# Local attention in a two-layer kernel on one core: one probabilities-times-V step per pair of heads, transposed probabilities kept in place of the probabilities, new issue orders

## The reference

```python
x = L0_attn_x
xn = _layernorm(x)
s = _L0_attn_ref(xn, ...)            # four quaternion/spectral sublayers, each with an MLP
g = _silu(_L0_ffn_ref(xn, ...))      # 8 experts, top 2
x = x + s * g
xn = _layernorm(x)
s = _L1_attn_ref(xn, W_qkv, W_out)   # the change is in here
g = _silu(_L1_ffn_ref(xn, ...))      # 32 experts, top 4 in 2 of 4 groups, and a shared one
x = x + s * g
```

```python
sim = jnp.einsum('bhwid,bhwjd->bhwij', bq, bk)      # 128 queries x 256 keys per window
sim = jnp.where(mask, mask_value, sim)
attn = jax.nn.softmax(sim, axis=-1)
out = jnp.einsum('bhwij,bhwjd->bhwid', attn, bv)
```

## Time and profile before

| | value |
|---|---|
| median of 3 runs | 4467.36 us (4463.34 to 4469.44) |
| the profiled execution | 4463.56 us |
| its span (first to last instruction) | 4461.7 us |
| mean granted TensorE clock | 0.967 of full |
| PE busy | 3924.9 us (88%), 18416 instructions |
| DVE busy | 3710.1 us (83%), 10482 |
| ACT busy | 3203.3 us (72%), 7121 |
| POOL busy | 1291.5 us (29%), 1520 |
| DMA, mean over the span | 33 GB/s |

### The profile page before, as it was taken

One profiled execution on the slowest core, in us unless ns is written; L12 is line 12 of the kernel. 1 busy time (PEld: TensorE's weight loads), 2 busy tenths in 40 slices (PEclk: granted clock), 3 DMA queues, 4 the chain that ended last, 5 costly groups with the idle time before them and its releaser, 6 DMA issues. The chain is left out here.

```text
span 4461.7 us, 62568 instructions
## 1 busy us (share of the span) xinstructions
PE 3924.9 (88%) x18416; PEld 2244.7 (50%) x18416; DVE 3710.1 (83%) x10482; ACT 3203.3 (72%) x7121; POOL 1291.5 (29%) x1520
## 2 busy tenths in 40 slices
PE   5668998999989999998999899999998998999978
PEld 3335555555555545555554555545555554554544
DVE  4769898898988889798888988889798888979854
ACT  2447778677776867777777776867777787777756
POOL 0123233222332322233232323322233332223321
PEclk8779999999999999999999999999999999999989
DMA  4011111011111111111111111101111111111100
GB/s 135 15 29 27 27 38 37 25 31 36 30 28 33 33 31 31 29 34 35 30 30 36 26 28 36 39 22 34 33 32 30 32 33 33 31 29 33 36 22 22
DMA packets 144425, 148.05 MB, mean 33 GB/s; under 512 B 27749, under 2 KB 107933, under 8 KB 143961
## 3 DMA queue, kind: packets, MB, share of 16 engines
q1 hardware_dynamic: 144088, 144.06, 12.4%
HBM read 22.32 MB, written 4.19 MB: 6 GB/s over the span
## 5 line engine op out<-in xcount | busy, mean ns | idle before, releaser
L633 POOL TENSOR_TENSOR rot<-rot,sinT 128x512 f32<-128x512 f32 x256 | 336.8, 1316 | 814.7 <-DMA rot<-raw 814.7
L955 DVE TENSOR_TENSOR acc<-acc,tmp 128x512 f32<-128x512 f32 x768 | 559.4, 732 | 8.1
L1387 PE MATMUL bC<-hu,w_d 128*128 128x512 f32 x1056 | 562.8, 615 | 2.8 <-DVE hu L1151 2.6
L605 POOL TENSOR_TENSOR veA<-mvA,epsT 128x2 f32<-128x2 f32 x290 | 83.5, 288 | 1631.7 <-DVE mvA L807 1629.1
L955 DVE TENSOR_TENSOR tmp<-comps 128x512 f32<-128x512 f32 x768 | 539.7, 708 | 7.4
L751 ACT ACTIVATE probs<-probs,nmax 128x256 f32<-128x256 f32 (+1 forms) x1024 | 480.5, 470 | 75.3 <-DVE nmax L1106 72.4
L779 ACT ACTIVATE s_h<-bG 128x512 f32<-128x512 f32 x528 | 314.8, 596 | 193.5 <-PE bG L1370 170.1
L1151 DVE TENSOR_TENSOR hu<-bU,s_h 128x512 f32<-128x512 f32 x528 | 359.7, 681 | 78.5 <-PE bU L1380 67.4
L624 POOL TENSOR_TENSOR comps<-comps 128x255 f32<-128x255 f32 (+1 forms) x384 | 268.7, 703 | 470.6 <-ACT comps L697 470.0
L1106 DVE CUSTOM_DVE_ANT_0 probs<-bT,maskb 128x256 f32<-128x256 f32 (+1 forms) x1024 | 344.9, 383 | 68.3 <-PE bT L1296 67.5
L1277 PE MATMUL bA<-acc,w_fc 128*128 128x256 f32 x1024 | 333.4, 416 | 42.0 <-ACT acc L715 32.5
(11 more groups left out here) (202 smaller groups left out, 8838.5 us busy)
## 6 DMA issues: line engine op xcount, KB each, us to landing
rot<-raw SPq DMA_DIRECT2D x1024, 64.0 KB, 2.0
comps<-comps SPq DMA_DIRECT2D x384, 120.0 KB
x_ld<-in_L_attn_x SPq DMA_DIRECT2D x66, 128.0 KB, 2.2
comps<-comps SPq DMA_DIRECT2D x384, 8.0 KB
out<-sums SPq DMA_DIRECT2D x16, 256.0 KB, 2.2
w_a<-in_L_attn_W_qkv SPq DMA_DIRECT2D x1, 1536.0 KB, 14.4
w_fc<-in_L_attn_fc_w SPq DMA_DIRECT2D x1, 1024.0 KB, 9.5
w_g<-in_L_ffn_w_gate SPq DMA_DIRECT2D x1, 1024.0 KB, 5.6
```

The source lines that it names most:

```text
L633: nc.gpsimd.tensor_tensor(rot[:, i, :], rot[:, i, :], sinT[:, :], ALU.mult).then_inc(sin_part, 1)
L955: V_.tensor_tensor(dst, i0, i1, op).then_inc(ham[h], 1)
L1387: ins = mm(bC[:, :], down, hu[:, :], start=u in (0, UNITS0), stop=u in (UNITS0 - 1, UNITS - 1))
```

## The change

`O` becomes one step per pair over all 512 columns, and the transposes of the reciprocals become a step `RT` of their own with its own bank. There are again 13 bank fillings per pair. `rinv` is one step (128x8 reciprocal, 128x512 spread), ACT's copy of the transposed reciprocals is one 128x512 copy, DVE's product one 128x512 multiplication. The tile `probsT` is gone: ACT writes the transposed probabilities over the probabilities themselves (`in_set`), in the two windows and the head that PE has just transposed. The semaphore `scaled` is gone: DVE waits for `O` on PE and for `RT` on ACT. The matmuls and transposes are the same in number and shape. The strings of all five engines are new.

```diff
-        out += [("rinv", p, 0), ("PT", p, 0), ("PT", p, 1), ("rinv", p, 1), ("O", p, 0), ("PT", p, 2), ("PT", p, 3), ("O", p, 1)]
+        out += [("PT", p, 0), ("PT", p, 1), ("rinv", p), ("PT", p, 2), ("PT", p, 3), ("RT", p), ("O", p)]
...
 ORDER = {
-    "pe": "uuuauabaubautbuuubuttutuuuuuutuuuututttuuuttuuuttaautuatauauuuatuababtuttauauauabubututbtububbut"
+    "pe": "uuuauababuauubtubututuututuuuutuuuuuutuuttutututaatuuuaauuttuuaauababutttauauauauubtbttububbttub"
...
-        probsT = sb("probsT", [P, 2, 4 * WIN])
...
+        def in_set(h, n):
+
+            return probs[:, h, 2 * n:2 * n + 2, :].rearrange("p w n -> p (w n)")
...
                     if t[0] == "PT":
                         t_ready(act, r, t)
                         at = P if t[2] < 2 else 0
-                        copy(probsT[:, t[2] % 2, at:], b[:, at:]).then_inc(t_sem(t), 1)
+                        copy(in_set(t[2] % 2, t[2] // 2)[:, at:], b[:, at:]).then_inc(t_sem(t), 1)
                     if t[0] == "rinv":
-                        w = slice(2 * t[2], 2 * t[2] + 2)
-                        act.wait_ge(rinved, r.b * (2 * HP) + (2 * t[1] + t[2] + 1))
-                        copy(sums[:, w, :].rearrange("p w (h d) -> p w h d", h=2),
-                             rinv[:, w, :].unsqueeze(3).to_broadcast([P, 2, 2, DH])).then_inc(spread, 1)
-                    if t[0] == "O":
+                        act.wait_ge(rinved, r.b * HP + (t[1] + 1))
+                        copy(sums[:, :, :].rearrange("p w (h d) -> p w h d", h=2),
+                             rinv[:, :, :].unsqueeze(3).to_broadcast([P, NW, 2, DH])).then_inc(spread, 1)
+                    if t[0] == "RT":
                         t_ready(act, r, t)
-                        copy(sums[:, 2 * t[2]:2 * t[2] + 2, :].rearrange("p w d -> p (w d)"), b[:, HT:S]).then_inc(scaled, 1)
+                        copy(sums[:, :, :].rearrange("p w d -> p (w d)"), b[:, :]).then_inc(t_sem(t), 1)
...
                     if t[0] == "rinv":
-                        w = slice(2 * t[2], 2 * t[2] + 2)
-                        if t[1:] == (0, 0):
+                        if t[1] == 0:
                             dve.wait_ge(stored, r.b * 16 + 16)
-                        dve.wait_ge(exped, r.b * (NW * HP) + (NW * t[1] + 2 * t[2] + 2))
-                        V_.reciprocal(rinv[:, w, :], rsum[:, w, :]).then_inc(rinved, 1)
+                        dve.wait_ge(exped, r.b * (NW * HP) + (NW * t[1] + NW))
+                        V_.reciprocal(rinv[:, :, :], rsum[:, :, :]).then_inc(rinved, 1)
                     if t[0] == "O":
-                        dve.wait_ge(scaled, r.b * (2 * HP) + (2 * t[1] + t[2] + 1))
-                        V_.tensor_tensor(OT[:, t[1] % 2, t[2] * HT:(t[2] + 1) * HT], b[:, 0:HT],
-                                         sums[:, 2 * t[2]:2 * t[2] + 2, :].rearrange("p w d -> p (w d)"),
+                        t_ready(dve, r, t)
+                        t_ended(dve, r, ("RT", t[1]))
+                        V_.tensor_tensor(OT[:, t[1] % 2, :], b[:, :], sums[:, :, :].rearrange("p w d -> p (w d)"),
                                          ALU.mult).then_inc(t_sem(t), 1)
...
+                    if t[0] == "RT":
+                        pe.wait_ge(spread, r.b * HP + (t[1] + 1))
+                        ins = transposes(b, [sums[:, w, :] for w in range(NW)])
                     if t[0] == "O":
 
-                        tiles = ((2, 1, 0, 2), (1, 0, 0, 1), (3, 3, 1, 1)) if t[2] else ((0, 1, 0, 2), (1, 3, 1, 1))
-                        for n, (key, at, to, wide) in enumerate(tiles):
-                            for h in range(2):
-                                mm(b[h * DH:(h + 1) * DH, to * WIN:(to + wide) * WIN], V[:, key, h, :],
-                                   probsT[:, h, at * WIN:(at + wide) * WIN], start=n == 0, stop=n == len(tiles) - 1)
-                        pe.wait_ge(spread, r.b * (2 * HP) + (2 * t[1] + t[2] + 1))
-                        ins = transposes(b[:, HT:S], [sums[:, 2 * t[2] + w, :] for w in range(2)])
+                        for half, tiles in enumerate((((0, 1, 0, 2), (1, 3, 1, 1)), ((2, 1, 0, 2), (1, 0, 0, 1), (3, 3, 1, 1)))):
+                            for n, (key, at, to, wide) in enumerate(tiles):
+                                for h in range(2):
+                                    ins = mm(b[h * DH:(h + 1) * DH, half * HT + to * WIN:half * HT + (to + wide) * WIN],
+                                             V[:, key, h, :], in_set(h, half)[:, at * WIN:(at + wide) * WIN],
+                                             start=n == 0, stop=n == len(tiles) - 1)
```

More of the change, by code:

```diff
@@ L96 @@
                  "fc0", "fc1", "fc2", "fc3", "mproj"},
-           "t": {"xn1_T", "route1", "q", "k", "V", "S", "PT", "O", "gates1_T", "out", "final_T"},
+           "t": {"xn1_T", "route1", "q", "k", "V", "S", "PT", "RT", "O", "gates1_T", "out", "final_T"},
            "u": {"gate", "weight", "down", "up"}, "r": set()},
@@ L100 @@
                   "prep_T", "gate_T", "gates0_T", "ln2_T", "fc0", "fc1", "fc2", "fc3"},
-            "t": {"xn1_T", "route1", "q", "k", "V", "S", "rinv", "PT", "O", "gates1_T"},
+            "t": {"xn1_T", "route1", "q", "k", "V", "S", "rinv", "PT", "RT", "gates1_T"},
             "u": {"gate", "down"}, "r": {"r0"}},
@@ L141 @@
-    "sp": "aabbabttttaatatbbbttaatatbbbttttaababbtbatt",
+    "pe": "uuuauababuauubtubututuututuuuutuuuuuuutttuttututaatuuuaauuttuuaauababutttauauauauubtbttububbttub"
+          "tuuububtutuutbtabuauttauattattattauttatttuuuuttautatbuabuuattubttbuububbubttuutuutubttubbuabtaut"
+          "auuutatattuatuuatuattuatuttbubtbuataubttbtbtabttbbtatuutttutbuutbubttubttutaatbtttuuutttbuuuuttu"
+          "uuutuuuutttuuuuuttuaubtautbtuttbaubatbaubabaubtabta",
+    "act": "uaabauabaaaabaabtbabbubbbtbtutabubtuttuauttttutattuatattaautaaaaaaataaabaubatbbbuttttuabtbbtutbt"
+           "bbbtubtbbbaatbtattaattttuttttuatbataauaataaaatbaubbtbbuttttatabutbbbtbbttbbbbtubbbataatuataatttt"
+           "tutttatbabatubttbtbaabattaatttaattbattbtbbbubbbbabtabtabbtubtttttutttttuuturttuttttttttabubababa"
+           "babua",
@@ new lines @@
+    "dve": "aubatbutaaubabauaaubabbabauauaubatuauaabatutattatauaabtbaburubbbbbbbrbuaabbaburtauarauaatturaata"
+           "aabbatubatataauaaauabuaabratbbbbbbtbbbbtutttbabattuaubbbbbabtbuaubaaaatatuuaaaaabbtatuutabaaaatb"
+           "uabuaabtbbbabububbbtbbbtbtbubttubaatbatbbuubtatatbbttbtuutaaaaabtabauuatbbbbbaabttbabatttuburrbt"
+           "bauauababauutbabubuttaubbutbatrabaubtbrubautttbtbaa",
+    "pool": "abtaabbbtatttttaabaatabtbbtbatatatabtbtabtbbaabattttatabtabbbbtttab",
+    "sp": "aabbttabttaattabbttbaattabbbttattababatbtbt",
@@ L348, in program @@
         exped = sem("exped")
-        rinved, spread, scaled = sem("rinved"), sem("spread"), sem("scaled")
+        rinved, spread = sem("rinved"), sem("spread")
         y_gated = sem("y_gated")
@@ L1307, in t_part @@
                     builds_on = {"route1": [("xn1_T",)],
-                                 "O": [("V",) + t[1:2]] + [("PT", t[1], 2 * t[-1] + k) for k in range(2)] if t[0] == "O" else [],
-                                 "out": [("O", 2 * t[-1] + k, n) for k in range(2) for n in range(2)] if t[0] == "out" else []}
+                                 "O": [("V",) + t[1:2]] + [("PT", t[1], k) for k in range(4)] if t[0] == "O" else [],
+                                 "out": [("O", 2 * t[-1] + k) for k in range(2)] if t[0] == "out" else []}
                     if t == ("q", 0):
```

## The result

| | before | after |
|---|---|---|
| median, range of four runs | 4468.4 us (4463.3 to 4471.0) | 4432.2 us (4430.1 to 4439.6) |
| ratio of the times, 95% interval | | 0.9923 (0.9906 to 0.9941) |
| span of the profiled execution | 4461.7 us | 4428.7 us |
| granted clock, mean | 0.967 | 0.970 |

The account below looks back on a forecast made before the run. PE was taken as the nearest bound, with DVE's lateness making most of its gaps. PE's 37 us and DVE's 22 us, half let through as 30 us, took 4463.6 to 4434 us; range 4395 to 4487.

Parts of the forecast that it names:

- PE's wait at the product: PE waiting for ACT's copies before the product with V: 56.1 us before, forecast to fall under 20.
- PE gives back 37 us: Two thirds of PE's 56.1 us wait before the product with V, taken as removed PE idle time.
- nothing to see: Rival, chance 0.14: PE's work sets the end and gaps return before other steps; 4463 us, within 9 us.
- PE's work: Matmuls and transposes on PE stay the same, so nothing was taken off PE's work.
- forecast 39.9: Upper-end fall of DVE's busy time from merged reciprocals and products: 148.9 removed less 109.0 added.
- counted 22: DVE's gain in capacity from merged reciprocals and products, 21.8 us by distances between instruction starts, taken as 22.
- ACT at nothing: ACT's merged copies (50.6 us less busy) and saved table loads (23.1 us) costed at nothing, covered by ACT's idle time.
- 18 table loads: Table loads on ACT that the new order saves, at 1.283 us each, 23.1 us.
- The round: A full round taken as 259.9 us from DVE's last steps, 15 to 16 times; about 258 us expected after.
- The slower rival: Chance 0.22: PE waits at RT for ACT's spread, 0.85 us in each of 128 steps, 109 us; 4489 us, or 4507.
- Half of 59 let through: PE's 37 and DVE's 22 us, halved to 30 us because an engine standing less arrives earlier at its next wait.
- A third of 96 us lost: Larger-gain rival, chance 0.18: PE's 56.1 and DVE's 39.9 us count fully, 4368 us, or 4395 with a third lost.

Follow-up runs that it names:

- the second profile: The changed kernel, unaltered, measured and profiled again: 4436.2 us, ratio 0.9932 to before; span 4437.5 us, PE busy 3912.6 us.
- The two splits on PE: The changed kernel with PE's product issued as two pieces, in all pairs (4500.4 us) or with pair 1 whole and pieces placed to avoid waits (4504.1 us).
- RT is early: New steps in the old order, with RT alone moved ahead on PE in all pairs and on ACT in seven: 4573.8 us, ratio 1.0239.
- five moves of RT or the product: New steps, old order: RT earlier 4573.8 us, also DVE's product later 4714.0, pair 7 alone 4576.2. Changed kernel: PE's product earlier 4577.4, DVE's later 4445.1.

## Why the prediction was right, point by point

The time, 4432 against 4434 us, was right, and so was the sign. The steps were not all right, and two errors stood against each other, so that the close number is in part luck.

- **PE's wait at the product: right in place, wrong in worth.** Forecast was a fall from 56.1 us to under 20; it fell to 2.3. The step "PE gives back 37 us" was mis-sized as a gain: PE's waits on DVE and ACT are 475.6 us before and 478.6 after, and all of its idle time fell by 8.7 us (11.9 in the second profile). In the full rounds it fell by 3 us. This is the rival "nothing to see" in its reason, that the gaps come back in front of other steps, though not in its time. In the last round the mechanism held: 15.3 us of wait went, and idle time fell by 10.9.
- **PE's work: the step that failed.** "Matmuls and transposes are the same, so nothing comes off its work". The same matmuls are busy for 24.3 us less in one profile and 12.3 in the other; with the clock taken out both give an estimated 16 to 17 us, about half of the gain. The earlier trace rows show one of the four groups of a pair, which was read for its wait alone; what a group holds PE for was never taken. The two splits on PE bear it out from the other side: +31.5 us of busy time each.
- **DVE: right in the number, by luck.** Busy time fell by 47.3 us for a forecast 39.9, the long product takes 683 ns for 681, the 8-column reciprocal 194 ns for the 170 that were taken. But the halves put back bring only 7.0 us of busy time, and the merged steps in the old order are 16.0 us above before: most of the fall belongs to the order. In time the halves cost 5 to 9 us, with some 10 us of noise, so the 11 us that half of the counted 22 come to are neither shown nor excluded.
- **ACT at nothing: not contradicted.** 62.7 us less busy for a forecast "some 70"; its halves put back cost 7 to 10 us, which the noise does not tell from nothing. The 18 table loads were not tried alone.
- **The round.** The prediction gave a full round as 259.9 us, from the last step of each sequence. The last round is short, so that a full one takes 264.4, and 262.9 after. By the same count as forecast it is (4425.4 - 559.4) / 15 = 257.7, "about 258". But nothing in the sum spoke of the last round, where 14.4 of the 33.0 us arose.
- **The slower rival.** Its wait, PE for the spread, is 9.3 us in place of 109. The reason given against it fits: the transposes themselves now wait for the exponentials, 32.4 us where it was 0.3, so the spread is seldom what comes last. Its ground, that a merged step loses what the halves overlapped, fits what is seen where the order is left as it was, though the cause of that loss stayed open: the same steps are slower by 2.25% there, and PE waits 70.4 us for the spread where RT is early. The rule of the Trainium skill that was weighed for it (Perfetto Trace Analysis, "Optimizing Scalar/DVE Operations") thus fits this merge in the old order, by the 98 us, and not in the new.
- **Half of 59 let through.** The factor has nothing behind it now: most of what it was applied to came back as waits, and what it left out, 16 to 17 us of PE's work, was over half of the 30.
- **Slips that change nothing.** By the string, 20 steps stand before the first half-products and not 21, and ten half-products had one to three, not nine. A third of 96 us lost leaves 4400 and not 4395.

**Still open.** Which places of the new order carry the 134 us between the same steps in the two orders. Of five moves of RT or the product, two cost some 140 us and three can't be told from nothing; none gained, so no single one of the waits that were moved holds the loss. The transposes written in place rather than to a tile of their own were not tried alone, nor was the merging on PE without that on DVE and ACT. Why the last round keeps the gain that the full ones lose again is read from one difference, that the first layer's work is missing there, and was not tried either.

## What to carry to other kernels

Count what an interruption costs on TensorE: four groups of a pair made into two took 0.21 to 0.27 us less, while a removed wait may come back in front of the next late step, as it did here in the full rounds. Profile a kernel twice before dividing a small gain into busy and idle time: two profiles of the same kernel differed by 12.0 us in PE's busy time, half of the 24.3 that the first had shown as gained. Put merged instructions back into halves before crediting them with a fall in busy time. Judge an edit to the steps only in an order made for it: the same steps ran at 4567 us in the old order and at 4432 in the new. Take the first and the last round of a pipelined program apart from the full ones before dividing.

## What the runs showed of the hardware

- The duration of one matmul depends on its neighbours in the queue. The transposes of `sums` take 304 ns in the mean in groups of two and 279 in groups of four [the groups above]; a group of two holds PE for 0.28 us, one of four for 0.44 at the least and 0.50 in the mean. A product group divided into 8 and 12 matmuls holds PE for 0.15 us longer, and the group of another width between the pieces took 0.63 instead of 0.43 us.
- The clock enters busy time: the same kernel had PE busy for 3900.6 us at a mean clock of 0.970 and for 3912.6 at 0.966.
- The same DVE instruction lasts longer or shorter by the order around it: 128x512 `raw<-raw,cosT` takes 783 and 789 ns in the mean in two kernels with the old order, 703 and 695 in two with the new.
- A DVE instruction halved cost little here: 256 more instructions made DVE's busy time 7.0 us longer, 27 ns each, though the product's halves take 414 ns each against 683 for the whole.
